# A fused attention and mixture-of-experts layer: expert places read beside v, and the last normalisation split anew between VectorE and GpSimd

## The chip, the core and the metric

The kernel runs on one core of a Trainium2 chip. The time is the device time of one execution in microseconds (us); the median of several executions is given. The engines are named TensorE (PE in the rows; PEld is its weight load), VectorE (DVE), ScalarE (ACT), GpSimd (POOL) and SyncE (SP, which here only issues copies).

## What is computed

Input x is 8 x 256 x 256 in float32, 2048 tokens of 256 features. With `ln` a normalisation over the last axis:

```
x = x + ln(attention(ln(x)))     # 16 query heads, 4 key/value heads of 128; q and k normalised
                                 # and rotated (rope); causal softmax; output projection
x = x + ln(ffn(ln(x)))
ffn: logits = x @ gate_w.T (8 experts); softmax, top 2, weights scaled to sum 1
     out  = sum over the 2 experts of weight * (silu(x @ w_gate) * (x @ w_up)) @ w_down    (176 wide)
     out += sigmoid(x @ shgate_w) * (silu(x @ shw_gate) * (x @ shw_up)) @ shw_down          (352 wide)
```

## The kernel before

Everything is one program per engine, with its order written out by hand; engines meet only at semaphores (`s_...`), each engine runs its own list strictly in order, and a wait in the list holds everything behind it. The float32 products run as three fp32r products of a high and a low part (`mm3`).

**The woven loop.** `for s in range(WOVEN)` (129 steps) carries the attention. A *unit* u (0 to 63) is one key/value head of one 128-token tile; it takes two steps. `qkv(u, y)` on TensorE writes q and k (y = 0: columns 0 to 511 of `pQ`; y = 1: columns 512 to 767, one more head and v). ScalarE squares them for the norm; VectorE's `rope(u, y)` multiplies them by the tables (L1430, L1435; semaphore `s_t2`) and splits v (L1437, `s_v`); GpSimd's `rope(u)` takes a root (L2006, L2008) and finishes with three 128x640 operations (L2020, L2023, L2030; semaphore `s_rope`). Heads follow some steps behind: `scores`, softmax on VectorE and ScalarE, `probs_T`, `pv`, `out_proj`.

**The router.** Tokens are given places in the experts' lists in three chunks of tiles (0 to 9, 10 to 13, 14 to 15). For chunk 0, inside the loop: VectorE finds the two best experts (`route_...`, s = 108 to 117), `route_count(0)` (s = 118; L1624, L1628) sums them, TensorE's `places(0)` (end of s = 118; L672, L679, ten small products into `pA`) makes running counts, `place_read(0)` (s = 119; L1653) reads them, `place_own(0)` (s = 120; L1659, L1662) and `place_ends(0)` (s = 122; L1667, L1669, L1670) write the slots (`s_slots`). One `pv` waits on `s_placed` because it writes the same PSUM bank `pA`. After its last rope GpSimd scatters rows to memory by these slots (L2113), two indirect copies a tile. Expert weights are loaded by SyncE from the moment that the last rope is done (`s_rope`), and converted by ScalarE's `ew_hi` (L1036).

**The feed-forward part and the last normalisation.** From 553 us on, items q walk through the tiles (`ffn(q)` on each engine): 39 routed tiles, then the last five shared ones. Under and behind these comes the end: eight pairs p of tiles, one each q (`PAIR`). For a pair: the two routed rows are added (`last_ysum` on GpSimd, L2147, for p < 5), the shared result is added (`last_sum`, L1731, VectorE; for p = 5 to 7 TensorE makes both sums in PSUM: `pair_results`, `pair_shared`, L755 to L760), `last_stats` (L1740, with L1536 in `norm_aggr`) gives mean and variance, `last_root` on GpSimd gives the scale `lr2` and the offset `nb2` in four operations (L2083, L2085, L2087, L2091), ScalarE's `last_apply` (L1136, semaphore `s_fapp`) applies them, `last_add` on VectorE (L1759) adds the result to x, and SyncE copies the pair out (L449, L452). Pairs 0 and 1, 2 and 3, 4 and 5 share a root, 6 and 7 have their own; pair 7 is scaled and added on VectorE (L1748, L1754) instead.

Names used below: u_lo(m) is L1572, u_act(m) L1568, both VectorE, per shared tile m; out_scale(b) L1491 and out_add(b) L1497; pv_lo L1471, probs_lo L1466; ln2_lo L1550; ew_lo L1510.

## Time and profile before

| what | value |
|---|---|
| median of 3 runs | 680.37 us (679.06 to 681.21) |
| the profiled execution | 683.07 us |
| its span, first to last instruction | 681.0 us |
| mean granted TensorE clock | 0.989 |
| busy: TensorE / VectorE / ScalarE / GpSimd | 631.6 / 567.2 / 564.5 / 552.6 us |

The profile takes one execution; its span leaves out the 2.07 us of start and end. A timeline row is the start of an instruction in us, its duration, engine, line, operation and tiles; where the engine was idle before it, the row ends with that time and with what ended it. Instructions of one engine overlap by some hundredths of a us where they do not depend on each other. A duration is the time from start to completion, waits inside the operation included.

### The profile page before, as it was taken

What the parts mean: (1) busy time and instruction counts of PE and PEld (TensorE: products, weight loads), DVE (VectorE), ACT (ScalarE), POOL (GpSimd) and SP (SyncE); (2) the same over time, 40 slices, a digit from 0 to 9 for tenths busy, and PEclk for the clock granted to TensorE, in tenths of its full rate; (3) what the DMA queues carried; (4) which work ended last, traced back from release to release, by engine and by line L of the source; (5) the groups of instructions that cost most, each with busy time, mean ns of one, the idle gap of its engine ahead of it and who ended that gap; (6) DMA issues with size and microseconds to landing.
All of it is one profiled execution on the core that took longest, in us unless ns stands there. A gap on an engine that the chain in (4) does not pass through costs nothing.

```text
span 681.0 us, 15537 instructions
## 1 busy us (share of the span) xinstructions
PE 631.6 (93%) x4430; PEld 581.0 (85%) x4430; DVE 567.2 (83%) x1925; ACT 564.5 (83%) x2175; POOL 552.6 (81%) x590
## 2 busy tenths in 40 slices
PE   3668999999999999999999999999799999999993
PEld 2557899999999999999999999899688888999981
DVE  6899999998989889888888889999978854555576
ACT  5779999999989999998999999999888535666643
POOL 5799889999999999999999998989866424566654
PEclk9789999999999999999999999999999999999998
DMA  8001113999530000000000000000436124444263
GB/s 336 15 1 33 30 73 118 334 334 276 3 47 1 1 2 2 1 1 2 1 2 1 2 1 2 1 1 25 142 116 203 55 81 116 123 131 119 70 256 124
DMA packets 50978, 54.20 MB, mean 80 GB/s; under 512 B 19824, under 2 KB 42608, under 8 KB 50768
## 3 DMA queue, kind: packets, MB, share of 16 engines
q1 hardware_dynamic: 47488, 43.84, 22.3%
q0 software_dynamic: 3408, 9.38, 3.8%
q8 instruction: 38, 0.62, 0.4%
q14 instruction: 44, 0.36, 0.2%
HBM read 23.76 MB, written 29.51 MB: 78 GB/s over the span
## 4 chain that ended last, share of the span: by engine, by line
POOL 52%; PE 25%; ACT 10%; DVE 6%; issue 4%; DMA 1%; another core or an unknown queue 0%; ACTq 0%; SPq 0%; DVEq 0%; POOLq 0%
POOL ropes L2030 11%; POOL ropes L2020 11%; POOL ropes L2023 9%; POOL rs L2008 9%; PE pQ L459 2%; PE pQ L461 2%; PE pQ L460 2%; POOL hrow L2044 2%; ACT ropes L980 2%; ACT P L995 2%; POOL osb L2051 2%; PE pO L459 2%; POOL rs L2006 2%; POOL lr L2008 1%; PE pO L460 1%
## 5 line engine op out<-in xcount | busy, mean ns | idle before, releaser
L459 PE MATMUL pQ<-W 128*128 128x512 f32 (+2 forms) x334 | 119.3, 357 | 9.6 <-DVE W L1389 5.2
L995 ACT ACTIVATE P<-P,nmx 128x128 f32<-128x128 f32 (+1 forms) x256 | 119.9, 500 | 0.0
L460 PE MATMUL pQ<-W 128*128 128x512 f32 (+2 forms) x334 | 114.4, 342 | 0.0
L461 PE MATMUL pQ<-W 128*128 128x512 f32 (+2 forms) x334 | 113.8, 341 | 0.0
L1003 ACT ACTIVATE P<-P,rinv 128x128 f32<-128x128 f32 (+1 forms) x256 | 107.0, 490 | 1.8 <-DVE rinv L1462 1.6
L2020 POOL TENSOR_TENSOR ropes<-ropes 128x640 f32<-128x640 f32 x63 | 99.2, 1575 | 6.7 <-DVE ropes L1435 6.7
L2030 POOL TENSOR_TENSOR ropes<-ropes 128x640 f32<-128x640 f32 x63 | 100.1, 1589 | 4.9
L980 ACT ACTIVATE ropes<-pQ 128x128 f32<-128x128 f32 x320 | 89.3, 308 | 13.6 <-POOL ropes L2030 7.6
L459 PE MATMUL pO<-W 128*128 128x256 f32 (+1 forms) x323 | 95.1, 295 | 5.4 <-DVE W L1471 3.9
L1466 DVE TENSOR_TENSOR W<-pP,W 128x384 fp32r<-128x384 f32 x128 | 70.2, 548 | 27.6 <-ACT W L1008 27.3
L460 PE MATMUL pO<-W 128*128 128x256 f32 (+1 forms) x323 | 91.5, 283 | 0.0
L461 PE MATMUL pO<-W 128*128 128x256 f32 (+1 forms) x323 | 91.2, 282 | 0.0
L2023 POOL TENSOR_TENSOR ropes<-ropes,rs 128x640 f32<-128x640 f32 x63 | 81.1, 1288 | 4.9
L2008 POOL TENSOR_TENSOR rs<-rs,half 128x5 f32<-128x5 f32 x64 | 77.3, 1207 | 5.3
L459 PEld LDWEIGHTS pQ<-W 128*128 128x128 f32 x334 | 65.3, 195 | 15.9 <-issue 4.5
L980 ACT ACTIVATION_READ_ACCUMULATOR ropes<-pQ 128x1 f32 x320 | 75.2, 241 | 0.0
L459 PEld LDWEIGHTS pO<-W 128*128 128x128 f32 x323 | 61.4, 190 | 12.9 <-DVE W L1471 7.0
L461 PEld LDWEIGHTS pQ<-W 128*128 128x128 f32 x334 | 65.2, 195 | 6.0
L1008 ACT ACTIVATE W<-pP 128x384 fp32r<-128x384 f32 x128 | 67.2, 525 | 2.6 <-PE pP L527 1.4
L460 PEld LDWEIGHTS pQ<-W 128*128 128x128 f32 x334 | 65.7, 197 | 2.9
L2142 POOL DMA_INDIRECT ys<-ropes x39 | 38.8, 995 | 34.1 <-ACT ropes L1131 27.1
L527 PE MATMUL pP<-const,P 128*128 128x128 f32 x384 | 63.2, 274 | 2.0 <-DVE W L1466 1.4
(268 smaller groups left out, 2205.7 us busy)
## 6 DMA issues: line engine op xcount, KB each, us to landing
xs<-stage SPq DMA_DIRECT2D x1, 17550.0 KB, 58.4
stage<-xs SPq DMA_DIRECT2D x39, 130.0 KB
ropes<-in_ew SPq DMA_DIRECT2D x8, 608.0 KB
stage<-in_wqkv SPq DMA_DIRECT2D x3, 768.0 KB, 9.1
stage<-ys SPq DMA_DIRECT2D x4, 512.0 KB, 6.3
ropes<-ys SPq DMA_DIRECT2D x4, 512.0 KB, 7.4
out<-X SPq DMA_DIRECT2D x7, 256.0 KB, 2.0
X<-in_wo SPq DMA_DIRECT2D x1, 1536.0 KB, 13.1
```

Of the source, the lines that this page charges most:

```text
L459: e.matmul(out, lh, rh, start=start, stop=False, skip_group_check=True)
L460: e.matmul(out, lh, rl, start=False, stop=False, skip_group_check=True)
L461: return e.matmul(out, ll, rh, start=False, stop=stop, skip_group_check=True)
L980: a = e.activation(t2[:, z, h * D:h * D + D], pQ[:, h * D:h * D + D], ACT.Square, accum_out=ss[:, z, h:h + 1])
L995: a = e.activation(P[:, z, span(t)], P[:, z, span(t)], ACT.Exp, bias=nmx[:, z, t:t + 1], scale=-1.0, accum_out=sums[:, z, t:t + 1])
L1003: a = e.activation(P[:, z, span(t)], P[:, z, span(t)], ACT.Copy, scale=rinv[:, z, t:t + 1])
L1008: e.activation(PT[:, 0, n % 2, :], pP[:, 0:384], ACT.Copy).then_inc(s_PThi, 1)
L1466: e.tensor_tensor(PT[:, 1, n % 2, :], pP[:, 0:384], f(PT[:, 0, n % 2, :]), ALU.subtract).then_inc(s_PT, 1)
L2008: e.tensor_tensor(dst, dst, half[:, 0:n], ALU.pow).then_inc(s_root, 1)
L2020: e.tensor_tensor(t1[:, z3, :], t1[:, z3, :], t2[:, z, :], ALU.add).then_inc(s_add, 1)
L2023: e.tensor_tensor(v3, v3, rs[:, z, :].unsqueeze(2).to_broadcast([128, 5, D]), ALU.mult).then_inc(s_mul, 1)
L2030: e.tensor_tensor(v3, v3, TB[:, t, :, :], ALU.add).then_inc(s_rope, 1)
```

## The change

Two independent parts.

1. **Chunk 0 of the router.** `places(0)` goes to TensorE's s = 119, ahead of `qkv(59, 1)`, and writes columns 768 to 847 of `pQ` instead of `pA`; the wait of `pv` on `s_placed` goes. `place_read(0)` goes into VectorE's `rope(59, 1)` at s = 120. `route_count(0)`, `place_own(0)` and `place_ends(0)`, seven operations, go out of the loop to behind `soft_rinv(120)`, ahead of `out_scale(6)`.
2. **The last normalisation.** `last_root` on GpSimd keeps the power alone (one operation for four). VectorE makes variance + eps (`last_var`, right behind the statistics) and, later, the offset (`last_nb`, one operation). The additions to x of pairs 1, 3 and 5 go to GpSimd (`last_add` there), those of 0, 2, 4 and 6 stay on VectorE but at other places.

Names:

```
-COUNT_PV = (COUNT0 - 12) // 2
+UPLACE = (COUNT0 + 1) // 2
+POOLADD = (1, 3, 5)
...
-                for (a, b), p in zip(CHUNKS, (pA, pS[1], pS[1]))]
+                for (a, b), p in zip(CHUNKS, (pQ[:, 768:1024], pS[1], pS[1]))]
```

TensorE, in `qkv`, `pv`, `places` (which moves up in the file, unchanged but for this wait) and the loop:

```
+                if u == UPLACE and y == 1:
+                    places(0)
...
-                if 2 * i + 13 == 119:
-                    e.wait_ge(s_placed, 1)
...
-                if c == 0:
-                    e.wait_ge(s_aT, COUNT_PV)
...
-                if s == COUNT0:
-                    places(0)
```

VectorE, in `rope`, in the loop and behind it:

```
+                if u == UPLACE and y == 1:
+                    place_read(0)
...
-                if s == 119:
-                    place_read(0)
...
-                if s == 118:
-                    route_count(0)
-                if s == 120:
-                    place_own(0)
-                if s == 122:
-                    place_ends(0)
...
             soft_rinv(120)
+            route_count(0)
+            place_own(0)
+            place_ends(0)
             out_scale(6)
```

VectorE, the last normalisation (`last_scale` now raises `s_fsum` instead of `s_fapp`, and `last_add_tile` waits for that):

```
+            def last_var(p, n):
+                z = slice(p % 4, p % 4 + n)
+                if p >= 4:
+                    e.wait_ge(s_fapp, p + n - 4)
+                else:
+                    e.wait_ge(s_h2row, NT)
+                e.wait_ge(s_aggr2, NB + p + n)
+                e.tensor_scalar(lr2[:, z, :], mv2[:, z, :, 1], 1.0, EPS, ALU.mult, ALU.add).then_inc(s_var2, 1)
+
+            def last_nb(p, n):
+                z = slice(p % 4, p % 4 + n)
+                e.wait_ge(s_lr2, NB + root_of(p) + 1)
+                e.scalar_tensor_tensor(nb2[:, z, :], mv2[:, z, :, 0], -1.0, lr2[:, z, :], ALU.mult,
+                                       ALU.mult).then_inc(s_nb2, 1)
...
                     if PAIR[q] < PPE:
                         last_sum(PAIR[q])
+                    if PAIR[q] == 4:
+                        last_nb(2, 2)
                     last_stats(PAIR[q])
+                    if PAIR[q] >= 6:
+                        last_var(PAIR[q], 1)
+                    elif PAIR[q] % 2 == 1:
+                        last_var(PAIR[q] - 1, 2)
...
-                p = PAIR.get(q - 2, 0)
-                if 0 < p < 6 and p % 2 == 1:
-                    last_add(p - 1)
-                    last_add(p)
+                p = PAIR.get(q, 0)
+                if p == 2:
+                    last_nb(0, 2)
+                elif p == 3:
+                    last_add(0)
                 elif p == 6:
-                    last_add(p)
+                    last_add(2)
+                    last_nb(4, 2)
                 elif p == 7:
-                    last_scale(p)
+                    last_nb(6, 1)
+                if PAIR.get(q - 1, 0) == 7:
+                    last_add(4)
+                    last_scale(7)
+                    last_add(6)
                     for t in range(2):
-                        last_add_tile(p, t)
+                        last_add_tile(7, t)
```

GpSimd, `last_root` whole as it was (-) and is, and its three additions, each behind the root of the same q:

```
             def last_root(p, n):
-                k = NB + root_of(p)
-                if p >= 4:
-                    e.wait_ge(s_fapp, p + n - 4)
-                else:
-                    e.wait_ge(s_h2row, NT)
                 z = slice(p % 4, p % 4 + n)
-                e.wait_ge(s_aggr2, NB + p + n)
-                e.tensor_scalar(lr2[:, z, :], mv2[:, z, :, 1], 1.0, EPS, ALU.mult, ALU.add).then_inc(s_var2, 1)
-                if p < NPAIR - 1:
-                    e.tensor_scalar(nb2[:, z, :], mv2[:, z, :, 0], -1.0, None, ALU.mult)
-                e.wait_ge(s_var2, k + 1)
+                e.wait_ge(s_var2, NB + root_of(p) + 1)
                 e.tensor_tensor(lr2[:, z, :], lr2[:, z, :], half[:, 0:2 * n].rearrange("p (a b) -> p a b", a=n),
                                 ALU.pow).then_inc(s_lr2, 1)
-                if p < NPAIR - 1:
-                    e.wait_ge(s_lr2, k + 1)
-                    e.tensor_tensor(nb2[:, z, :], nb2[:, z, :], lr2[:, z, :], ALU.mult).then_inc(s_nb2, 1)
+
+            def last_add(p):
+                e.wait_ge(s_fapp, p + 1)
+                e.tensor_tensor(X[:, 2 * p:2 * p + 2, :], X[:, 2 * p:2 * p + 2, :], yl[p][:, :, 0:HID],
+                                ALU.add).then_inc(s_ysum, 1)
...
+                if p == 3:
+                    last_add(1)
+                elif p == 6:
+                    last_add(3)
+                elif p == 7:
+                    last_add(5)
```

SyncE copies the pairs out in their order still, waiting for the engine that adds each (`s_ysum` for 1, 3 and 5, `s_fres` for the others).

How the change moves instructions. On VectorE just behind the loop stood, from soft_max(121) through soft_rinv(120) to the rinv of head 121:

```order
L1456 ISA P,nmx<-pS,P 128x128
L1456 ISA nmx 128x1
L1462 RECIPROCAL rinv<-sums 128x2
L1491 TENSOR_SCALAR osb<-osb,mv,lr 128x256 x2
L1471 TENSOR_TENSOR W<-pA,W 128x512
L1497 TENSOR_TENSOR X<-X,osb 128x512
L1462 RECIPROCAL rinv<-sums 128x2
```

and now stands:

```order
L1473 RECIPROCAL rinv<-sums 128x2
L1635 TENSOR_REDUCE stage<-oh 128x8
L1639 CAST csum<-stage 128x8
L1662 TENSOR_TENSOR stage<-stage 128x160
L1665 TENSOR_REDUCE stage<-stage 128x20
L1670 TENSOR_SCALAR stage<-stage 128x10
L1672 COPY stage<-stage 128x10
L1673 CAST slots<-stage 128x2x10
L1502 TENSOR_SCALAR osb<-osb,mv,lr 128x256 x2
L1482 TENSOR_TENSOR W<-pA,W 128x512
L1508 TENSOR_TENSOR X<-X,osb 128x512
```

The seven operations of the router's chunk 0 (count, own place, slots) lie between soft_rinv and out_scale (L1491, now L1502), and pv_lo (L1471, now L1482) comes seven operations later.

On VectorE in the last normalisation, from last_stats of pair 3 to the additions of pairs 2 and 3, stood (L1731 last_sum, L1740 and L1536 last_stats, L1759 last_add):

```order
L1572 TENSOR_TENSOR W<-pP,W 128x384
L1731 TENSOR_TENSOR ropes<-ropes 128x2x256
L1740 BN_STATS st<-ropes 128x6 x2
L1536 BN_AGGR mv<-st 128x2 x2
L1759 TENSOR_TENSOR X<-X,stage 128x512 x2
L1731 TENSOR_TENSOR ropes<-ropes,P 128x2x256
L1740 BN_STATS st<-ropes 128x6 x2
L1536 BN_AGGR mv<-st 128x2 x2
L1740 BN_STATS st<-pS 128x6 x2
L1536 BN_AGGR mv<-st 128x2 x2
L1759 TENSOR_TENSOR X<-X,ropes 128x512 x2
```

Now, from u_lo(15) on (L1754 last_var, L1759 last_nb, L1777 last_add; L1734 last_sum, L1743 and L1547 last_stats):

```order
L1583 TENSOR_TENSOR W<-pP,W 128x384
L1759 SCALAR_TENSOR_TENSOR nb<-mv,lr 128x4
L1734 TENSOR_TENSOR ropes<-ropes 128x2x256
L1743 BN_STATS st<-ropes 128x6 x2
L1547 BN_AGGR mv<-st 128x2 x2
L1754 TENSOR_SCALAR lr<-mv 128x4
L1777 TENSOR_TENSOR X<-X,stage 128x512
L1734 TENSOR_TENSOR ropes<-ropes,P 128x2x256
L1759 SCALAR_TENSOR_TENSOR nb<-mv,lr 128x4
L1743 BN_STATS st<-ropes 128x6 x2
L1547 BN_AGGR mv<-st 128x2 x2
L1743 BN_STATS st<-pS 128x6 x2
```

Pair 1's addition is gone, the variance stands ahead of pair 0's addition, and an offset each stands ahead of last_sum(3) and ahead of last_stats(4). In the same way a last_var stands right behind last_stats(1), ahead of u_lo(14).

On GpSimd behind its last indirect copies stood (L2147 last_ysum, the rest last_root of pairs 0, 2, 4 and 6):

```order
L2147 TENSOR_TENSOR stage<-stage 128x2x256 x2
L2147 TENSOR_TENSOR ropes<-ropes 128x2x256 x3
L2083 TENSOR_SCALAR lr<-mv 128x4
L2085 TENSOR_SCALAR nb<-mv 128x4
L2087 TENSOR_TENSOR lr<-lr,half 128x4
L2091 TENSOR_TENSOR nb<-nb,lr 128x4
L2083 TENSOR_SCALAR lr<-mv 128x4
L2085 TENSOR_SCALAR nb<-mv 128x4
L2087 TENSOR_TENSOR lr<-lr,half 128x4
L2091 TENSOR_TENSOR nb<-nb,lr 128x4
```

and now stands, to the end of the program (L2103 the power, L2108 last_add):

```order
L2165 TENSOR_TENSOR stage<-stage 128x2x256 x2
L2165 TENSOR_TENSOR ropes<-ropes 128x2x256 x3
L2103 TENSOR_TENSOR lr<-lr,half 128x4 x2
L2108 TENSOR_TENSOR X<-X,stage 128x512
L2103 TENSOR_TENSOR lr<-lr,half 128x4
L2103 TENSOR_TENSOR lr<-lr,half 128x2
L2108 TENSOR_TENSOR X<-X,ropes 128x512
L2103 TENSOR_TENSOR lr<-lr,half 128x2
L2108 TENSOR_TENSOR X<-X,ropes 128x512
```

Pair 1's addition follows the second power, pair 3's the power of pair 6, pair 5's the power of pair 7.

## Rows read from the trace of the kernel before

**Rows 1.** Busy us (x instructions) in a stretch: PE, PEld, DVE, ACT, POOL; clock, DMA.

```profile
456.00:470.00 14.00, 14.00 (x105) 13.22 (x105) 12.63 (x49) 13.55 (x60) 12.84 (x12) 1.00 0.09 30
```

**Rows 2.** Timeline of GpSimd, 442 to 484 us: start, duration, instruction, [idle before, its releaser].

```profile
442.76 1.17 POOL L2008 TENSOR_TENSOR rs<-rs,half 128x5 f32<-128x5 f32 x1
443.89 1.56 POOL L2020 TENSOR_TENSOR ropes<-ropes 128x640 f32<-128x640 f32 x1
...
450.50 1.55 POOL L2020 TENSOR_TENSOR ropes<-ropes 128x640 f32<-128x640 f32 x1 [0.65 <-DVE ropes L1435]
...
458.81 1.55 POOL L2020 TENSOR_TENSOR ropes<-ropes 128x640 f32<-128x640 f32 x1 [0.68 <-DVE ropes L1435]
...
472.87 1.56 POOL L2020 TENSOR_TENSOR ropes<-ropes 128x640 f32<-128x640 f32 x1 [0.48 <-DVE ropes L1435]
...
482.95 1.54 POOL L2030 TENSOR_TENSOR ropes<-ropes 128x640 f32<-128x640 f32 x1
```

**Rows 3.** Timeline of VectorE, 657 to 677 us.

```profile
657.48 1.10 DVE L1731 TENSOR_TENSOR stage<-stage,ropes 128x512 f32<-128x512 f32 x1
...
659.40 0.25 DVE L1536 BATCH_NORM_AGGREGATE mv<-st 128x2 f32<-128x6 f32 x2
659.57 0.52 DVE L1572 TENSOR_TENSOR W<-pP,W 128x384 fp32r<-128x384 f32 x1
...
662.41 0.56 DVE L1572 TENSOR_TENSOR W<-pP,W 128x384 fp32r<-128x384 f32 x1 [0.18 <-ACT W L1092]
...
664.56 1.26 DVE L1759 TENSOR_TENSOR X<-X,stage 128x512 f32<-128x512 f32 x2
665.73 0.68 DVE L1731 TENSOR_TENSOR ropes<-ropes,P 128x512 f32<-128x512 f32 x1
...
668.39 0.25 DVE L1536 BATCH_NORM_AGGREGATE mv<-st 128x2 f32<-128x6 f32 x2
...
676.21 0.76 DVE L1754 TENSOR_TENSOR X<-X,stage 128x256 f32<-128x256 f32 x2
```

**Rows 4.** Timeline of VectorE, 443 to 460 us: three of the seven moved operations.

```profile
443.97 1.51 DVE L1628 CAST csum<-stage 128x8 fp32r<-128x8 f32 x1
...
451.29 0.95 DVE L1659 TENSOR_TENSOR stage<-stage 128x160 f32<-128x160 f32 x1
...
459.60 0.80 DVE L1667 TENSOR_SCALAR stage<-stage 128x10 f32<-128x10 f32 x1
```

**Rows 5.** Timeline of VectorE at 545 us.

```profile
545.21 0.16 DVE L1667 TENSOR_SCALAR stage<-stage 128x2 f32<-128x2 f32 x1
```

**Rows 6.** Timeline of GpSimd, 655 to 668 us.

```profile
655.41 2.62 POOL L2147 TENSOR_TENSOR ropes<-ropes 128x512 f32<-128x512 f32 x2 [0.34 <-DMA ropes<-ys]
659.34 1.28 POOL L2147 TENSOR_TENSOR ropes<-ropes 128x512 f32<-128x512 f32 x1 [1.31 <-DMA ropes<-ys]
...
661.51 1.04 POOL L2087 TENSOR_TENSOR lr<-lr,half 128x4 f32<-128x4 f32 x1
...
665.88 1.42 POOL L2087 TENSOR_TENSOR lr<-lr,half 128x4 f32<-128x4 f32 x1
```

**Rows 7.** Timeline of TensorE at 454 us.

```profile
454.17 0.47 PE L459 MATMUL pA<-W 128*128 128x512 f32 x1 [0.29 <-DVE W L1550]
```

**Rows 8.** Timeline of VectorE, 482 to 485 us: what follows the last soft_rinv.

```profile
482.16 2.49 DVE L1491 TENSOR_SCALAR osb<-osb,mv,lr 128x256 f32<-128x256 f32 x2
484.57 0.68 DVE L1471 TENSOR_TENSOR W<-pA,W 128x512 fp32r<-128x512 f32 x1
```

**Rows 9.** Timeline of ScalarE at 489 us.

```profile
488.80 1.22 ACT L1036 ACTIVATE W<-ropes 128x1216 fp32r<-128x1216 f32 x1 [0.94 <-DMA ropes<-in_ew]
```

**Rows 10.** Timeline of ScalarE at 672 us.

```profile
671.62 1.09 ACT L1136 ACTIVATE ropes<-ropes,nb,lr 128x256 f32<-128x256 f32 x2 [1.93 <-POOL nb L2091]
```

**Rows 11.** Timeline of GpSimd at 528 us.

```profile
528.25 0.91 POOL L2008 TENSOR_TENSOR lr<-lr,half 128x2 f32<-128x2 f32 x1
```

**Rows 12.** Timeline of VectorE at 528 us.

```profile
528.60 1.16 DVE L1510 TENSOR_TENSOR W<-ropes,W 128x960 fp32r<-128x960 f32 x1
```

More of the change, by code:

```diff
@@ L447, in _ @@
             for p in range(NPAIR - 1):
-                e.wait_ge(s_fres, p + 1)
+                if p in POOLADD:
+                    e.wait_ge(s_ysum, PPE + POOLADD.index(p) + 1)
+                else:
+                    e.wait_ge(s_fres, p // 2 + 1)
                 e.dma_start(out_d[:, 2 * p:2 * p + 2, :], X[:, 2 * p:2 * p + 2, :]).then_inc(s_out, 16)
             for m in (NT - 2, NT - 1):
-                e.wait_ge(s_fres, m - NT + NPAIR + 2)
+                e.wait_ge(s_fres, m - NT + 2 + NPAIR - len(POOLADD))
                 e.dma_start(out_d[:, m:m + 1, :], X[:, m:m + 1, :]).then_inc(s_out, 16)
@@ L475, in ln1_T, with places @@
                 p.then_inc(s_ln1T, 1)
+            def places(c):
+                a, b = CHUNKS[c]
+                e.wait_ge(s_oh, c + 1)
+                if c > 0:
+                    e.wait_ge(s_csum, c)
+                if c == 1:
+                    e.wait_ge(s_max, NHEAD)
+                elif c == 2:
+                    e.wait_ge(s_placed, 2)
+                out = pPos[c]
+                p = e.matmul(out, uptri[:, :], oh[:, a:b, :], start=True, stop=False,
+                             skip_group_check=True)
+                if c > 0:
+                    p = e.matmul(out, ones,
+                                 csum[:, c - 1:c, :].to_broadcast([128, b - a, NE]), start=False, stop=False,
+                                 skip_group_check=True)
+                for t in range(b - a - 1):
+                    p = e.matmul(out[:, t + 1:b - a, :], ones,
+                                 oh[:, a + t:a + t + 1, :].to_broadcast([128, b - a - 1 - t, NE]), start=False,
+                                 stop=t == b - a - 2, skip_group_check=True)
+                p.then_inc(s_pos, 1)
             def qkv(u, y):
@@ L658, in u_down @@
                 p.then_inc(s_udown, 1)
-            def places(c):
-                a, b = CHUNKS[c]
-                e.wait_ge(s_oh, c + 1)
-                if c > 0:
-                    e.wait_ge(s_csum, c)
-                if c == 0:
-                    e.wait_ge(s_aT, COUNT_PV)
-                elif c == 1:
-                    e.wait_ge(s_max, NHEAD)
-                else:
-                    e.wait_ge(s_placed, 2)
-                out = pPos[c]
-                p = e.matmul(out, uptri[:, :], oh[:, a:b, :], start=True, stop=False,
-                             skip_group_check=True)
-                if c > 0:
-                    p = e.matmul(out, ones,
-                                 csum[:, c - 1:c, :].to_broadcast([128, b - a, NE]), start=False, stop=False,
-                                 skip_group_check=True)
-                for t in range(b - a - 1):
-                    p = e.matmul(out[:, t + 1:b - a, :], ones,
-                                 oh[:, a + t:a + t + 1, :].to_broadcast([128, b - a - 1 - t, NE]), start=False,
-                                 stop=t == b - a - 2, skip_group_check=True)
-                p.then_inc(s_pos, 1)
             def counts():
@@ L1421, in rope_end, with place_read @@
                 e.tensor_tensor(v3, v3, TB[:, u % 2, :, :], ALU.add).then_inc(s_rope, 1)
+            def place_read(c):
+                a, b = CHUNKS[c]
+                e.wait_ge(s_pos, c + 1)
+                if c == LASTC:
+                    e.wait_ge(s_cnt, 1)
+                e.tensor_tensor(place[c], pPos[c], ebase.unsqueeze(1).to_broadcast([128, b - a, NE]),
+                                ALU.add).then_inc(s_placed, 1)
             def rope(u, y):
@@ L1646, in ends @@
                 return rows[:, a:b, col:col + 1].rearrange("p t c -> p (t c)")
-            def place_read(c):
-                a, b = CHUNKS[c]
-                e.wait_ge(s_pos, c + 1)
-                if c == LASTC:
-                    e.wait_ge(s_cnt, 1)
-                e.tensor_tensor(place[c], pPos[c], ebase.unsqueeze(1).to_broadcast([128, b - a, NE]),
-                                ALU.add).then_inc(s_placed, 1)
             def place_own(c):
```

6 lines of the change are left out of this document (3 added, 3 removed).

## The prediction

> **What bounds the kernel.** I read the chain of waits first. It runs through GpSimd's rope operations, the last of which ends at 484.49 us [rows 2], which suggests GpSimd as the bound of the woven loop. The busy time by stretch says otherwise: in the 14 us from 456 to 470, TensorE is busy for all 14.00, ScalarE for 13.55, VectorE for 12.63 and GpSimd for 12.84 [rows 1]. So the loop's pace is TensorE's, and GpSimd waits here and there for a rope that VectorE delivers late: 0.65 us at unit 59, 0.68 at 60 and 0.48 at 62 [rows 2]. At the very end the order turns round: from 657 us on VectorE works almost without a gap until its last root, then root, application and addition follow one another, and the last addition ends at 676.97 [rows 3].
>
> A third thing decides this change: operations of VectorE and GpSimd keep each other out of SBUF. The cast of 8 numbers a row, L1628, took 1.51 us, from 443.97 to 445.48, and GpSimd's L2020 ran from 443.89 to 445.45 [rows 2, 4]. L1659 (two SBUF inputs) took 0.95 and ended behind the L2020 that started at 450.50; L1667 (one input, strided) took 0.80 and ended behind the one that started at 458.81 [rows 2, 4]. The same operation on two numbers took 0.16 where nothing was in its way [rows 5]. last_sum(1) took 1.10, of which the free one has 0.68, next to GpSimd's last_ysum that ended at 658.03: so the way was free at 657.90, 0.13 before that end [rows 3, 6]. I use 0.13 throughout. What reads PSUM or is a statistic isn't held.
>
> **Part 1, in the loop.** The ten small products of places(0) move by less than a step in a list in which TensorE has no gap; their cost stays where it was. VectorE loses seven operations, three of which took 1.51 + 0.95 + 0.80 [rows 4]; the other four are short. But VectorE isn't the bound: the one gap of TensorE that they made is the 0.29 at 454.17, a pv that waited for ln2_lo (L1550), late behind place_own [rows 7]. GpSimd's waits at 59 and 60 shrink, and the time is waited at 62 instead, where VectorE itself waits for ScalarE and TensorE. I take **-0.3**. Bounds: 0, and -1.8, the sum of the three waits.
>
> **Part 1, behind the loop.** The seven operations now stand at 482.16, ahead of out_scale(6), while GpSimd is in its last rope operations. out_scale(6) itself was held there: 2.49 us for two short passes, to 484.65, when GpSimd's last rope had ended at 484.49 [rows 2, 8]. The count and the cast fit ahead of it, as one pass did; the product with two inputs is held to 484.36. After that come it and a reduction (some 0.25 each), three small ones (0.1 from start to start, the 0.16 of [rows 5] with its overlap) and both passes of out_scale instead of one (484.65 - 484.36 = 0.3): 0.8 + 0.3 = 1.1 us, so pv_lo(58) starts at 485.7 and not 484.57. Behind it are out_proj(116), probs_T(119) and ScalarE's probs_hi(119); then ScalarE waits anyway, 0.94 us, for the expert weights, whose load only the last rope releases [rows 9]. That covers most of the 1.1. GpSimd's first scatter waits for the slots, some 0.7 later, and its root for ln2 follows four scatters later. The scatter wait isn't in the trace of before. I take **+0.3** for both; bounds 0 (the load covers all) and +0.9 (the scatters pass it on whole).
>
> **Part 2, the end of the kernel.** Times on the clock of before.
> 1. last_var(0) is issued at 659.69, behind the aggregate that ends at 659.65. GpSimd's last_ysum(4) runs from 659.34 to 660.62 [rows 3, 6]. So it is held to 660.49 and u_lo(14) starts at 660.56, not 659.57: **+0.99**. Bounds 0.1 and 1.0.
> 2. u_lo(15) waits for ScalarE, which waits for TensorE's work on tiles 14 and 15: 662.41 becomes 663.40. last_nb(0) adds 0.15, so all from last_sum(3) on is late by 1.14. ScalarE's first application starts as much later, although the root is done.
> 3. The additions of pairs 0 and 1 started at 664.56 and took 1.26 [rows 3]. With 1.14, the wait for the last aggregate's end and last_var(2), 0.1 each, pair 0's starts at 665.9; pair 1's is gone, so last_sum(4) follows at 666.5 instead of 665.73.
> 4. The power of pair 2 has to wait for the addition, to 666.45, and takes 1.04 [rows 6] (before, it took 1.42 behind last_sum(4) [rows 6]): done at 667.49. last_nb(2) stands in VectorE's list ahead of last_stats(4) and waits for it. GpSimd's next operation is pair 1's addition, which waits for nothing any more and starts before the power has ended, as L2020 at 443.89 started 0.04 before the end of its root, L2008 [rows 2]. It takes what last_ysum takes, 1.28 [rows 6], and holds VectorE's two-input offset until 668.61. last_stats(4) starts at 668.75; before, it could when last_sum(4) was through, at 666.45. So last_stats(5) ends at 670.94 and not 668.64 [rows 3]: **+2.30** in all. Bound below: the offset slips in first, and it is +1.2.
> 5. From there the path is shorter. Before, 2.98 us passed from the end of last_stats(5) (668.64) to ScalarE's next application (671.62) [rows 3, 10]. Now: last_var(4), the power at 671.30 to 672.34, under it last_stats(6), then last_add(2) and last_nb(4), so 673.06, 2.12 after 670.94. **-0.86**.
> 6. The rest: last_var(7) comes at 674.04 into pair 3's addition on GpSimd (673.48 to 674.76), held to 674.63; last_nb(6); the power of pair 7 behind last_add(4), done at 676.1; last_scale(7) to 677.1; last_add(6), 0.2 held by pair 5's addition, to 677.9; the two last additions to about 678.6. Before: 676.97. The part behind ScalarE's application is 0.2 longer than before, since the chain now goes over GpSimd's list. The end of part 2 is thus **+1.65** (2.30 - 0.86 + 0.2).
>
> The last copies out leave closer together than before; I price that at nothing and leave it to the range.
>
> **The sum.** -0.3 + 0.3 + 1.65 = +1.65. Against the profiled execution of 683.07 this is 684.7; it lay 2.7 above the median of 680.37, and the median becomes **682.0**. A measurement of this kernel can tell about 0.3%, 2.04 us, from no change: the limits are 678.3 and 682.4. The forecast is no change that can be told, on the slow side.
>
> L1510, with two SBUF inputs, started at 528.60 inside a power of 528.25 to 529.16 and took 1.16, and the power 0.91 [rows 11, 12]: it wasn't held to the power's end, or 529.03 + 1.1 would stand there. So the sum goes without such waits. The Trainium skill has a rule that speaks against this change (SBUF — State Buffer, "Who interferes with whom"): of a GpSimd instruction and a VectorE one with two SBUF inputs, or in the fast mode of tensor_scalar, copy and cast, the first holds the shared ports for its whole instruction. For the long additions the rows agree; for the power they don't. By the rule the sum would be that of the first rival.
>
> **Rivals.**
> - **Powers hold the ports too (slower).** Against it are [rows 11, 12], one case only, with a power of two numbers; for it, that the longer additions do. Then last_sum(4) is held behind the power of pair 2, and pair 1's addition and last_nb(2) follow 0.5 later; last_nb(4) is held 0.6 behind the power of pair 6, and last_sum(2) 0.1 behind the first: +1.2, in all +2.85, 683.2. It decides once a power holds for over 0.4 us, when the sum passes 2.04.
> - **The small ones slip through.** last_var(0) isn't held (it has four numbers a row, where L1667 had ten), and last_nb(2) gets in ahead of the addition. Then 1.0 and 1.1 go: +1.65 - 2.1 = -0.45, 679.9. For it: one of out_scale's two passes found its way between two of GpSimd's operations [rows 8]. Against: L1667, strided too, was held [rows 4].
> - **GpSimd's rope chain is the bound of the loop after all**, and the three waits (1.8) go whole: 1.5 more gain than taken, 680.5, or 678.4 together with the rival before. For it is the chain of waits; against it that TensorE has no gap [rows 1].
> - **The late slots cost more.** GpSimd's scatters are released one by one by VectorE and ScalarE waits for the root behind them; if what lies behind has no slack, +1.2 comes on top of the 0.3: 683.2.
>
> **How the numbers follow.** The forecast 0.45; powers hold 0.15; small ones slip 0.20; rope chain 0.12; late slots 0.08. Around 682.0, with part 1 from -0.6 to +0.9 against the 0 taken and part 2 from +0.9 to +2.3, a good third of the forecast lies above 682.4 (0.16), and nearly all of the first and last rival (0.20): slower 0.36. Below 678.3 is half of the rope case's better half and little of the slipping one: faster 0.07. Within: 0.57. The range 679.3 to 683.9 holds the slipping case and both slow ones with some room.
>
> **What would show it.** Right: last_var(0) of some 0.9 us at 659.7, ending with last_ysum(4); last_nb(2) of over 1 us, ending 0.1 before pair 1's addition on GpSimd; last_stats(4) over 2 us later against last_stats(0) than before; the time from last_stats(5) to the next application 2.1 instead of 3.0; TensorE's gap before pv at the place of 454.17 gone and GpSimd's wait at unit 62 grown; the product of place_own long. Wrong: if last_var(0) and last_nb(2) take 0.2 each, part 2 has no loss. If GpSimd's last rope ends over 1 us earlier than 484.5, the loop was GpSimd's. If last_sum(4) is over 1 us beside a power, the first rival holds.

## The result, and the profile after

The changed kernel takes 682.33 us (median of 20 runs, 680.41 to 683.91), the kernel before in the same comparison 680.53 us: a ratio of 1.0022, with a 95% interval from 1.0013 to 1.0032, or 1.5 us slower (0.9 to 2.2). The forecast was 682.0 and no change that can be told, on the slow side. The number came out right. One step behind it did not, as the experiments show.

The profiled execution took 681.8 us, with a span of 679.8, which is less than the 681.0 of the one profiled before. So ends of work in the two traces can't be compared by the clock. I compare distances between two places of one trace. Timeline of VectorE in the changed kernel, 655 to 675 us (L1754 last_var, L1759 last_nb, L1777 last_add, L1583 u_lo, L1743 last_stats, L1734 last_sum):

```profile
655.84 1.23 DVE L1754 TENSOR_SCALAR lr<-mv 128x4 f32<-128x4 f32 x1
656.98 0.54 DVE L1583 TENSOR_TENSOR W<-pP,W 128x384 fp32r<-128x384 f32 x1
...
657.88 0.68 DVE L1734 TENSOR_TENSOR ropes<-ropes 128x512 f32<-128x512 f32 x1
...
660.32 0.15 DVE L1759 SCALAR_TENSOR_TENSOR nb<-mv,lr 128x4 f32<-128x4 f32 x1
...
662.33 0.68 DVE L1777 TENSOR_TENSOR X<-X,stage 128x512 f32<-128x512 f32 x1
662.93 0.68 DVE L1734 TENSOR_TENSOR ropes<-ropes,P 128x512 f32<-128x512 f32 x1
663.98 1.15 DVE L1759 SCALAR_TENSOR_TENSOR nb<-mv,lr 128x4 f32<-128x4 f32 x1 [0.37 <-POOL lr L2103]
665.05 0.74 DVE L1743 BATCH_NORM_STATS2 st<-ropes 128x6 f32<-128x256 f32 x2
...
666.18 0.76 DVE L1743 BATCH_NORM_STATS2 st<-pS 128x6 f32<-128x256 f32 x2
...
670.48 0.68 DVE L1754 TENSOR_SCALAR lr<-mv 128x2 f32<-128x2 f32 x1
...
672.42 1.00 DVE L1766 TENSOR_SCALAR stage<-pT,mv,lr 128x256 f32<-128x256 f32 x2 [0.60 <-POOL lr L2103]
673.34 0.83 DVE L1777 TENSOR_TENSOR X<-X,stage 128x512 f32<-128x512 f32 x1
674.10 0.75 DVE L1772 TENSOR_TENSOR X<-X,stage 128x256 f32<-128x256 f32 x2
```

The same stretch on GpSimd (L2165 last_ysum, L2103 the power, L2108 last_add):

```profile
654.42 2.63 POOL L2165 TENSOR_TENSOR ropes<-ropes 128x512 f32<-128x512 f32 x2 [1.15 <-DMA ropes<-ys]
657.15 1.04 POOL L2103 TENSOR_TENSOR lr<-lr,half 128x4 f32<-128x4 f32 x1
662.50 1.38 POOL L2103 TENSOR_TENSOR lr<-lr,half 128x4 f32<-128x4 f32 x1 [4.31 <-DVE lr L1754]
663.85 1.26 POOL L2108 TENSOR_TENSOR X<-X,stage 128x512 f32<-128x512 f32 x1
...
669.87 1.26 POOL L2108 TENSOR_TENSOR X<-X,ropes 128x512 f32<-128x512 f32 x1
671.24 1.15 POOL L2103 TENSOR_TENSOR lr<-lr,half 128x2 f32<-128x2 f32 x1
672.36 1.26 POOL L2108 TENSOR_TENSOR X<-X,ropes 128x512 f32<-128x512 f32 x1
```

- Two small operations take over a microsecond, as forecast. last_var(0) ends at 657.07 with last_ysum (657.05). last_nb(2) ends at 665.13 with GpSimd's addition of pair 1 (665.11), which had started 0.03 before the end of the power (663.88). The free last_nb(0) takes 0.15.
- last_sum(2), with two SBUF inputs, started at 657.88, inside the power of 657.15 to 658.19, and took its free 0.68. last_sum(4) ran from 662.93 to 663.61, wholly inside the power of 662.50 to 663.88, and took 0.68 too. Neither power held VectorE. That second power itself, which began beside last_add(0) (662.33 to 663.01), took 1.38 instead of 1.04.
- Before, the time from last_stats(0) (655.65) to last_stats(5) (667.59) was 11.94 us. Now it is 652.16 to 666.18, or 14.02: +2.08 against the forecast +2.30. From the end of last_stats(5), 667.23, to ScalarE's next application at 669.45 there are 2.22 us instead of the 2.98 of [rows 3, 10].

From last_stats(0) to the end of VectorE's last addition there were 21.32 us ([rows 3]: 676.97) and are 22.69: +1.37. That isn't all. The last GpSimd operation of the kernel before, from its timeline:

```profile
673.85 1.05 POOL L2087 TENSOR_TENSOR lr<-lr,half 128x2 f32<-128x2 f32 x1
```

It ended at 674.90, 6.10 us before the span's end of 681.0. GpSimd's last operation now ends at 673.62, 6.18 before the end of 679.8. VectorE's last addition ended 4.03 us before the end of the span and now ends 4.95 before it. The experiments had to say which of the two counts.

The loop, in busy us by engine for 456 to 470 us (columns as in [rows 1]), then GpSimd's waits at units 59, 60 and 62:

```profile
456.00:470.00 14.00, 14.00 (x107) 13.30 (x106) 11.84 (x46) 13.55 (x58) 13.07 (x11) 1.00 0.09 29
```

```profile
451.30 1.56 POOL L2045 TENSOR_TENSOR ropes<-ropes 128x640 f32<-128x640 f32 x1 [0.39 <-DVE ropes L1446]
...
459.47 1.55 POOL L2045 TENSOR_TENSOR ropes<-ropes 128x640 f32<-128x640 f32 x1 [0.53 <-DVE ropes L1446]
...
473.55 1.56 POOL L2045 TENSOR_TENSOR ropes<-ropes 128x640 f32<-128x640 f32 x1 [0.47 <-DVE ropes L1446]
...
483.67 1.58 POOL L2055 TENSOR_TENSOR ropes<-ropes 128x640 f32<-128x640 f32 x1
485.74 1.24 POOL L2131 DMA_INDIRECT xs<-stage,slots  x1 [0.49 <-DVE slots L1673]
```

VectorE is less busy (11.84 instead of 12.63), TensorE as full as ever, and the waits at units 59 and 60 shrink from 0.65 and 0.68 to 0.39 and 0.53. That at unit 62 stays (0.48, now 0.47). TensorE's gap of [rows 7] is gone. The moved operations behind the loop, on VectorE:

```profile
483.53 0.31 DVE L1662 TENSOR_TENSOR stage<-stage 128x160 f32<-128x160 f32 x1
483.87 0.32 DVE L1665 TENSOR_REDUCE stage<-stage 128x20 f32<-128x160 f32 x1
484.11 1.17 DVE L1670 TENSOR_SCALAR stage<-stage 128x10 f32<-128x10 f32 x1
...
485.99 0.68 DVE L1482 TENSOR_TENSOR W<-pA,W 128x512 fp32r<-128x512 f32 x1
```

The product (L1662) slipped in between two GpSimd operations, and the reduction behind it (L1665) wasn't held either. L1670, a tensor_scalar, ended at 485.28, 0.03 behind the last rope's end at 485.25; with the 0.16 that it takes when free [rows 5], it was held to 485.12. pv_lo(58) starts 0.74 after that end, where it was 0.08 in [rows 2, 8].

### The profile page after: what moved, and what is told of

The parts are those of the page before. It is cut to its first block, busy times and chain, and to the rows that moved or that the text cites. A ratio compares the mean times of both kernels' runs of the same rounds, so it can differ in the third digit from the quotient of the medians.

```text
span 679.8 us, 15535 instructions
## 1 busy us (share of the span) xinstructions
PE 630.5 (93%) x4430; PEld 580.9 (85%) x4430; DVE 566.6 (83%) x1931; ACT 565.2 (83%) x2175; POOL 554.4 (82%) x580
## 4 chain that ended last, share of the span: by engine, by line
POOL 63%; PE 20%; issue 6%; ACT 6%; DVE 3%; DMA 1%; SPq 0%; DVEq 0%; POOLq 0%; ACTq 0%
POOL ropes L2045 14%; POOL ropes L2055 14%; POOL ropes L2048 12%; POOL rs L2033 11%; POOL hrow L2069 3%; POOL osb L2076 2%; POOL rs L2031 2%; PE pQ L464 2%; POOL lr L2033 2%; PE pQ L466 2%; PE pQ L465 2%; ACT ropes L981 2%; PE pO L464 1%; PE pA L735 1%; PE pT L707 1%
## 5 line engine op out<-in xcount | busy, mean ns | idle before, releaser
L532 PE MATMUL pT<-const,ropes 128*128 128x128 f32 x320 | 58.0, 280 | 8.3 <-DVE W L1456 7.6
```

## The experiments

Besides the two kernels themselves there were twelve runs, of ten new kernels and once more of the two, each timed against the kernel before on the same chip. "Tail" below is the time from last_stats(0) to the end of VectorE's last addition. "x to G" runs from the start of the last x_lo (639.06 in the trace of before, 635.37 in that of the changed kernel) to the end of GpSimd's last operation; it contains the whole end of the kernel, waits for the gathered rows included. "G to end" and "V to end" run from GpSimd's and VectorE's last ends to the span's end.

| kernel | ratio to before (95%) | x to G | G to end | V to end |
|---|---|---|---|---|
| before, first profile | | 35.84 | 6.10 | 4.03 |
| changed | 1.0022 (1.0013 to 1.0032) | 38.25 | 6.18 | 4.95 |
| p1: part 1 alone | 1.0006 (0.9994 to 1.0018) | 36.36 | 6.16 | 4.08 |
| p2: part 2 alone | 1.0034 (1.0019 to 1.0050) | 38.46 | 6.16 | 4.94 |
| w1 | 1.0024 (1.0008 to 1.0039) | 37.20 | 6.15 | 4.93 |
| v0 | 1.0021 (1.0009 to 1.0033) | 37.33 | 6.17 | 4.95 |
| a0: before again | 0.9994 (0.9981 to 1.0008) | 35.85 | 6.16 | 4.09 |
| after2: changed again | 1.0025 (1.0012 to 1.0038) | 38.21 | 6.12 | 4.90 |
| both | 1.0005 (0.9991 to 1.0018) | 36.55 | 6.14 | 4.92 |
| best | 1.0002 (0.9990 to 1.0013) | 35.61 | 6.08 | 4.87 |
| nc: two copies left out | 1.0015 (0.9992 to 1.0038) | 38.18 | 6.16 | 4.94 |
| lc: before, copies late | 1.0004 (0.9982 to 1.0026) | 36.39 | 6.12 | 4.05 |
| best2 | 0.9955 (0.9932 to 0.9978) | 34.92 | 6.09 | 3.61 |
| gp: before, two powers more | 1.0038 (1.0019 to 1.0057) | 37.76 | 6.17 | 5.86 |

How far does x to G vary by itself? Where the end is that of the kernel before it was 35.84, 35.85, 36.36 (p1) and 36.39 (lc), and 35.99 in gp without its two additional powers. In p1 last_sum(1) was held beside a last_ysum (1.62 us instead of 0.68), which makes its tail 22.12. So a difference of 0.5 us between two of these distances can be chance; the 2.4 us between the kernel before and the changed one isn't.

**p1 and p2, the parts alone.** Both are the kernel before with some hunks of the diff above; p1, in its core, then p2:

```diff
+                if u == UPLACE and y == 1:
+                    places(0)
...
+            route_count(0)
+            place_own(0)
+            place_ends(0)
             out_scale(6)
```

```diff
+POOLADD = (1, 3, 5)
...
+            def last_var(p, n):
...
+            def last_nb(p, n):
```

> Part 1 alone on the kernel before: places(0) beside v and rope(59), the count, own slot and ends behind the last rope; the end of the kernel as it was. My theory: the gap of TensorE and the late slots cancel, so the time is that of the kernel before within 0.5 us (ratio 1.000), and the whole loss of the change lies in part 2. If the late slots are what costs (rival), this kernel is 1 to 1.8 us slower than the one before. If GpSimd's rope chain was the bound, it is 1.2 to 1.8 us faster. In the trace: GpSimd's waits at units 59 and 60 shorter, the first scatter some 0.3 us further behind the last rope.

> Part 2 alone on the kernel before: GpSimd's last roots as the power alone, the additions of pairs 1, 3 and 5 on GpSimd; the loop as it was. My theory: all of the loss is here, 1.3 to 1.8 us slower than the kernel before (ratio 1.0019 to 1.0026), and the stretch from last_stats(0) to the last addition is 22.6 to 23.0 us where it was 21.3. If the late slots are what costs, this kernel takes the time of the one before.

Part 1 alone can't be told from the kernel before, part 2 alone costs 2.3 us (1.3 to 3.4). The loss is in part 2. Its tail is 22.68 us, as forecast, and yet the 2.3 us lie above the forecast 1.3 to 1.8, though the interval reaches down to them.

**w1, the wait at last_nb(2).**

```diff
                 if p == 3:
+                    e.wait_ge(s_nb2, NB + 2)
                     last_add(1)
```

> The changed kernel with one wait more: GpSimd's last_add(1) waits until last_nb(2) is done, so it can't hold the ports against it. My theory: last_nb(2) takes 0.15 us instead of 1.15, last_stats(4) starts 0.9 us earlier against last_stats(0), and the kernel is 0.7 to 1.0 us faster than the changed one (about 0.9 us above the kernel before). If last_nb(2) is long because it waits for the power and not because of the addition, nothing changes.

VectorE, then GpSimd's addition in w1:

```profile
664.38 0.16 DVE L1759 SCALAR_TENSOR_TENSOR nb<-mv,lr 128x4 f32<-128x4 f32 x1 [0.37 <-POOL lr L2103]
664.46 0.74 DVE L1743 BATCH_NORM_STATS2 st<-ropes 128x6 f32<-128x256 f32 x2
```

```profile
664.62 1.27 POOL L2108 TENSOR_TENSOR X<-X,stage 128x512 f32<-128x512 f32 x1 [0.34 <-DVE nb L1759]
```

The operation that took 1.15 takes 0.16, the same inputs and the same wait for the power ahead of it. Only the addition beside it is gone. The tail is 21.70 instead of 22.69. The ratio, 1.0024, doesn't show the microsecond; its interval of 1 us to either side doesn't exclude it either.

**v0, the wait at last_var(0).**

```diff
-                    elif PAIR[q] % 2 == 1:
+                    elif PAIR[q] % 2 == 1 and PAIR[q] > 1:
                         last_var(PAIR[q] - 1, 2)
...
                 p = PAIR.get(q, 0)
+                if p == 1:
+                    last_var(0, 2)
```

> The changed kernel with last_var(0) issued one step later, behind u_act(15), where GpSimd's last_ysum(4) is through. My theory: last_var(0) takes 0.2 us instead of 1.23, u_lo(14) starts 1.0 us earlier against last_stats(0), and the kernel is 0.7 to 1.1 us faster than the changed one; that also shows in an earlier last_stats(3). If what follows u_lo(14) waits for ScalarE anyway (rival: the 1.0 is hidden), the time stays within 0.3 us of the changed kernel's.

```profile
656.07 0.23 DVE L1754 TENSOR_SCALAR lr<-mv 128x4 f32<-128x4 f32 x1
```

0.23 instead of 1.23, and a tail of 21.68: another 1.0 us, not hidden by ScalarE. Again the ratio is too coarse to show it.

**a0, after2, both, best.** The two kernels once more, beside two that build on w1 and v0. both has the edits of both. best has also the addition of pair 3 on VectorE:

```diff
-POOLADD = (1, 3, 5)
+POOLADD = (1, 5)
...
                 if PAIR.get(q - 1, 0) == 7:
+                    last_add(3)
                     last_add(4)
...
-                elif p == 6:
-                    last_add(3)
```

> The kernel before once more, for a second profile of it and as a measure of what two sets of runs of one kernel differ by. My theory: the 3 us of ScalarE waits put down to another core or an unknown queue, at 506 to 511 us, were a mark of that one profiled execution; from ew_hi(0) to the second slots there are some 25.5 us here instead of 28.6, while the stretch from last_stats(0) to the last addition is again 21.3 (up to 22.1, as in the run with part 1 alone). If those waits belong to the kernel before, 28.6 comes back. The ratio should be 1.000, with 0.001 to either side.

> The changed kernel once more, on the same chip as the two kernels that build on it. My theory: 1.0025 times the kernel before, and from last_stats(0) to the last addition 22.7 us again.

> The changed kernel with both waits taken away: last_var(0) one step later, and GpSimd's last_add(1) behind last_nb(2). My theory: each took 1.0 us off the end of the kernel by itself (22.69 to 21.70 and 21.68 from last_stats(0) to the last addition), and they add: 20.7 us, the time 1.7 to 2.0 us below the changed kernel and at or just below that of the kernel before (ratio 0.999 to 1.001). If one of them only moves a wait to the other's place, 21.7 stays.

> Both waits taken away, and the addition of pair 3 on VectorE, between last_nb(6) and last_add(4), where VectorE waits 0.60 us for the last root anyway. My theory: last_var(7) takes 0.2 us instead of 0.68, the last power isn't queued behind an addition, and from last_stats(0) to the last addition there are 19.9 to 20.1 us: 0.6 to 0.8 less than with both, and 1 us less than the kernel before (ratio 0.998). If VectorE's added 0.68 us isn't hidden by the wait for the root, it is as long as with both.

a0 settles a side question. From ew_hi(0) to the second slots it has 25.31 us, where the first profile of this same program had 28.61, with 3.04 us in its chain put down to "another core or an unknown queue". The changed kernel has 25.45. These waits came with that execution and not with the kernel, which is why its span was the longer one although its median is lower. after2 repeats the changed kernel: 1.0025, tail 22.76. Beside it on the same chip, both is at 1.0005: the two waits together are worth some 1.4 us by the timer and 1.7 us by x to G.

The tail of both is 21.47, and not 20.7: there a last_ysum started late and held last_sum(1) for 1.67 us instead of 0.68, a wait of 1.0 that isn't among the two taken away. best comes out at 20.15 us of tail, just above the forecast 19.9 to 20.1, with these on VectorE:

```profile
668.20 0.17 DVE L1754 TENSOR_SCALAR lr<-mv 128x2 f32<-128x2 f32 x1
668.27 0.15 DVE L1759 SCALAR_TENSOR_TENSOR nb<-mv,lr 128x2 f32<-128x2 f32 x1
668.34 1.28 DVE L1777 TENSOR_TENSOR X<-X,ropes 128x512 f32<-128x512 f32 x2
669.62 0.99 DVE L1766 TENSOR_SCALAR stage<-pT,mv,lr 128x256 f32<-128x256 f32 x2
```

last_var(7) is free, and the wait for the last root has gone whole behind the addition. But with a tail 1.1 us shorter than in a0 (21.23), best is level with the kernel before (1.0002), and not at 0.998. Here the forecasts failed, and the table's last columns say where: in every kernel with part 2 so far the span goes on 4.9 us behind VectorE's last addition, in those without it 4.1.

**nc and lc, are it the copies out?** My first reading of the 0.8 us was that four copies (two of 256 KB, two of 128) now leave together and share the DMA engines. nc is the changed kernel without the copies of pairs 5 and 6, so it leaves those rows of the output unwritten. lc is the kernel before with those two copies held back. nc, then lc:

```diff
-            for p in range(NPAIR - 1):
+            for p in range(NPAIR - 3):
                 if p in POOLADD:
...
-            e.wait_ge(s_out, 16 * (NPAIR + 1))
+            e.wait_ge(s_out, 16 * (NPAIR - 1))
```

```diff
-                e.wait_ge(s_fres, p + 1)
+                e.wait_ge(s_fres, p + 1 if p < 5 else NPAIR)
```

> The changed kernel without the copies out of pairs 5 and 6 (those rows of the output are not written); all else as it is. In all runs with part 2 the span ends 4.9 us behind VectorE's last addition, in those with the end of the kernel before 4.1, and the last copies take 2.1 instead of 1.8 us to land. My theory since those runs: four copies (256, 256, 128, 128 KB) now leave within 1.5 us and share the DMA engines, which move some 387 GB/s without a gap, so the last lands later. Then here the copy of the last tile lands after 1.8 us and the span ends 4.1 us or less behind the last addition, 0.8 us less than the changed kernel in all. If the 0.8 us is something else of part 2 (a rival), 4.9 us stays.

> The kernel before with one thing changed: SP issues the copies out of pairs 5 and 6 only when tile 14's last addition is done, so that they leave together with those of the last two tiles. No engine waits for them. My theory: 768 KB at 387 GB/s are 2.0 us from the first packet on, where the last tile's copy alone was through 1.4 us after its issue; the issues of four copies follow at 0.45 us each. The last copy lands 1.0 to 1.5 us later than before, and the span ends 5.1 to 5.6 us behind the last addition instead of 4.1: 1.0 to 1.5 us slower than the kernel before (ratio 1.0015 to 1.002). If copies close together cost nothing, as the prediction had it, nothing changes.

The reading falls, twice. How long the last tiles' two copies took to land (the line's own view, changed kernel, then nc, then lc):

```profile
DMA to landing us min/median/max: 2.1/2.1/2.2
```

```profile
DMA to landing us min/median/max: 1.7/1.8/1.8
```

```profile
DMA to landing us min/median/max: 2.1/2.2/2.3
```

So copies close together do take 0.3 to 0.4 us longer, as thought. Both expectations reckon with some 387 GB/s without a gap. The packets of the 256 KB copies come near it (2048 bytes in a median of 86 ns on each of 16 DMA engines, 381 GB/s); while the changed kernel's last four copies ran together, from 675.0 to 676.5, it was 358 GB/s. But the span doesn't end with them: nc still has 4.94 us behind VectorE's last addition, and lc, whose last copy is issued at 681.99, 1.04 after VectorE's last end, still has 4.05. What does stay the same in all thirteen profiles so far, that of best2 below included, is the distance from GpSimd's last end to the end of the span, 6.08 to 6.18 us. In the changed kernel GpSimd's last operation isn't the last root any more; it is the addition of pair 5, 1.26 us long, behind it.

**best2.** best, with pairs 1 and 2 added by GpSimd and pairs 4 and 5 by VectorE ahead of the scale. It was made to spread the copies; it also makes the last root GpSimd's last operation again.

```diff
-POOLADD = (1, 5)
+POOLADD = (1, 2)
...
-                    last_add(2)
+                    last_add(3)
                     last_nb(4, 2)
...
-                    last_add(3)
                     last_add(4)
+                    last_add(5)
...
                     last_add(1)
-                elif p == 7:
-                    last_add(5)
+                    last_add(2)
```

> The version with both waits taken away, with GpSimd adding pairs 1 and 2 and VectorE pair 3 in the place of pair 2, and pairs 4 and 5 ahead of last_scale(7), so that the copies out of pairs 3, 4 and 5 leave earlier. My theory: last_var(4) is held 0.3 us by the addition of pair 2, and the addition of pair 5 costs VectorE 0.3 to 0.6 ahead of the scale, so that the stretch from last_stats(0) to the last addition is 20.5 us, 0.4 more than with pair 3 alone on VectorE; but the span ends 4.1 to 4.3 us behind it instead of 4.9. In all 0.3 us below that version and 1 us below the kernel before (ratio 0.9985 to 0.9995). If the copies weren't what cost, it is 0.4 us slower than that version.

```profile
675.97 1.14 POOL L2106 TENSOR_TENSOR lr<-lr,half 128x2 f32<-128x2 f32 x1 [0.83 <-DVE lr L1754]
```

The tail is 20.46 (20.5 was expected), but the span ends 3.61 us behind it and not 4.1 to 4.3: it ends 6.09 behind this power, at 683.2. The ratio is 0.9955 (0.9932 to 0.9978), the only interval here that lies wholly below 1. x to G gives 0.9 us against the first profile, 0.9986, which is just outside that interval; against lc, whose end is that of the kernel before on the same chip (36.39), it gives 1.5 us. On the chip of this comparison the kernel before took 685.8 us and single runs scattered more widely; that best2 is faster than the kernel before is measured; by how much is not settled. The changed kernel itself wasn't timed on that chip; nc, which is nearly the same, was at 1.0015 (0.9992 to 1.0038).

**gp, the test of the new reading.** The kernel before, with two powers on GpSimd behind the last root, whose results nobody reads:

```diff
                 if p < NPAIR - 1:
...
+                else:
+                    for d in range(2):
+                        e.wait_ge(s_lr2, k + 1)
+                        e.wait_ge(s_nb2, k + d)
+                        e.tensor_tensor(nb2[:, z, :], lr2[:, z, :],
+                                        half[:, 0:2].rearrange("p (a b) -> p a b", a=1),
+                                        ALU.pow).then_inc(s_nb2, 1)
```

> The kernel before with two more powers of two numbers a row behind GpSimd's last root; their results are read by nobody, and a power hasn't held VectorE in any run. In all thirteen profiles the span ends 6.08 to 6.18 us behind the end of GpSimd's last operation, while it ends 3.6 to 4.9 us behind VectorE's last addition. My theory: the program's end waits for GpSimd, so the two powers (some 1.1 us each, 2.1 to 2.4 us together) come whole on the span: 6.1 us behind the second of them, some 6.3 us behind VectorE's last addition, and the time is 2.0 to 2.4 us above the kernel before (ratio 1.003). If VectorE's end or the last copies set the span (rival, and what the prediction took), nothing changes: the span ends 4.1 us behind the last addition, and 4 us behind the last power.

GpSimd, VectorE, and the span:

```profile
677.82 1.04 POOL L2087 TENSOR_TENSOR lr<-lr,half 128x2 f32<-128x2 f32 x1
678.94 1.69 POOL L2096 TENSOR_TENSOR nb<-lr,half 128x2 f32<-128x2 f32 x2
```

```profile
680.18 0.76 DVE L1754 TENSOR_TENSOR X<-X,stage 128x256 f32<-128x256 f32 x2
```

```profile
core 0: 686.8 us, clock 0.978
```

The two powers took 1.69 together, and with the 0.08 ahead of them GpSimd ends 1.77 us later. The span ends 6.17 behind them, and 5.86 instead of 4.1 behind VectorE's last addition: +1.77. Nothing that computes the output waits for these powers, VectorE ends before the span's end by more than ever, and the time is 2.6 us longer (1.3 to 3.9). The end of GpSimd's list sets the end of the span.

The trace also shows what lies between. Behind its own list each engine has some instructions that the program gets at its end; they stand under the line that encloses the whole program (`with ExitStack() as ctx:`, L117 of the kernel before and of gp) and aren't counted as busy. From that line's view, kernel before, then gp (an engine's name with a q is its sequencer; nanoseconds, then the start in us):

```profile
L117 POOLq EVENT_SEMAPHORE  x2: 17/17/17, 680.8 to 680.9; - x2
L117 POOLq DRAIN  x1: 6985/6985/6985, 673.8 to 673.8; - x1
L117 DVEq DRAIN  x1: 797/797/797, 676.2 to 676.2; - x1
L117 SPq DRAIN  x1: 7/7/7, 679.1 to 679.1; - x1
L117 DVEq EVENT_SEMAPHORE  x1: 21/21/21, 681.0 to 681.0; - x1
```

```profile
L117 POOLq DRAIN  x1: 6622/6622/6622, 679.9 to 679.9; - x1
L117 SPq DRAIN  x1: 7/7/7, 683.0 to 683.0; - x1
```

GpSimd's DRAIN lasts until 680.8, 5.9 us behind the end of its last power (674.90), and in gp until 686.5, again 5.9 behind (680.63). VectorE's is over at 677.0, and SyncE's at 679.1, just behind the landing of the last copy. The semaphore instructions of all engines come only after GpSimd's. So GpSimd arrives last, and it does in all fourteen profiles: SyncE, which waits for the last copy, is done 1.7 us ahead of it in the kernel before and 0.4 in lc.

## Why the prediction was right, and where it was wrong

**Where the loss is: right.** Part 2 carries it, part 1 is about nothing.

**Part 1 in the loop, -0.3: right.** From the start of unit 46's L2020 (354.53 in the trace of before) to the end of the last rope there are 129.64 to 129.93 us in the nine kernels with part 1 and 129.96 to 130.29 in the five without: means of 129.75 and 130.11, -0.36. The way to it was in part another: I expected GpSimd's wait at unit 62 to grow as those at 59 and 60 shrank, and it stayed. The two shrank by 0.41 us together and TensorE lost its gap of 0.29, and the gain fits either; the runs don't show which of the two engines sets the pace of the loop.

**Part 1 behind the loop, +0.3: right in sum, the terms were too large.** I put pv_lo(58) 1.2 us behind the last rope's end; it came at 0.74, since L1662 slipped in and not it but L1670 was held. The first scatter came 0.49 behind the rope instead of 0.19, +0.3 and not +0.7. From the last rope's end to the last x_lo the two undisturbed kernels without part 1 on the faster chips (a0, p2) have 150.30 and 150.13, the seven with it 150.12 to 150.79, mean 150.37: some +0.15, inside their own scatter.

**Part 2, step 1 (+0.99): right.** last_var(0) took 1.23, and v0 took exactly 1.0 out of the tail.

**Steps 2 to 4 (+2.30 at last_stats(5)): right**, 2.08. w1 shows the cause: the addition and not the power in front of it.

**Step 5 (-0.86): right**, 2.22 us instead of the forecast 2.12, so -0.76.

**Step 6: wrong, and with it what I took for the end.** "The rest: ... the two last additions to about 678.6. Before: 676.97 ... The end of part 2 is thus +1.65." VectorE's end did come as worked out (+1.37). But I had read from the chain of waits that the kernel ends with VectorE's last addition and the copy behind it. The 4 us behind that were never asked about. gp, nc and lc show that GpSimd's last end and 6.1 us fixed set the span's end. Counted from there, part 2 has three terms. The last power ends 20.23 us behind last_stats(0) instead of 19.25 and 19.16: +1.0. The addition of pair 5 is queued behind it: +1.2. And some +0.15 come ahead of last_stats(0). The sum is +2.4 (38.25 against 35.85), where I had +1.65. In my list this addition appeared as "0.2 held by pair 5's addition", a price on VectorE; on its own engine I gave it none.

**The copies out, priced at nothing: right**, though for no reason that I had. They take longer (2.1 instead of 1.8 us to land), but SyncE, which waits for them, is done ahead of GpSimd's DRAIN.

**Why the number was right all the same.** By x to G and the loop the change costs 2.4 - 0.36 + 0.15 = 2.2 us; measured are 1.5 (0.9 to 2.2) and, again, 1.7 (0.8 to 2.6). The forecast 1.65 lies in both intervals, and so, at the edge or inside, does 2.2. Runs of 12 don't part them. That p1 and p2 sum to 2.7 and the change to 1.6 is in the same scatter. The forecast had 0.7 us too little for part 2 (1.65 for 2.4) and was still within 0.2 us of the measured 1.5 and 1.7: as far as this goes, that the number fits is luck.

**The rivals.** Powers hold the ports: fallen, last_sum(2) beside the first power and last_sum(4) inside the second took 0.68 each. Here the trace decides against the rule of the Trainium skill that whichever of GpSimd and VectorE issues first keeps the shared ports for its whole instruction (SBUF — State Buffer, "Who interferes with whom"), as far as powers go. The long additions follow it: w1 and v0 priced each at 1.0. Small ones slip through: fallen for both operations it named, though L1662 did slip in. Rope chain as the bound, with all three waits gained: fallen, p1 isn't 1.2 us faster; but the waits didn't go (1.8 us before, 1.4 now), so this doesn't show that the chain isn't the bound. Late slots: p1's interval alone reaches to 1.2 us slower, where that rival begins; the 0.15 us from the last rope to the last x_lo speak against it.

## What to carry to other kernels

Ask first what ends the span, and look at every engine's last operation and at the DRAIN behind it, not only at the one that writes the output: the chain of waits ended at a VectorE addition here, while work put at the end of GpSimd's list, which nobody waited for, cost its whole length. Of work moved to another engine count its price there as well as what it holds elsewhere, and where a long GpSimd operation can start just ahead of a tiny one on VectorE, order them: a 0.15 us operation that loses by 0.1 us waits for all of it. When the timer can't tell 1 us, as here, distances inside one trace can, and they have to be checked by a kernel that moves only the suspected end.

## What was not expected of the hardware

- The span ends 6.08 to 6.18 us behind GpSimd's last operation in all fourteen profiles, over spans from 676.9 to 686.8 us (the spread of 0.1 comes from the rounding of the span). 5.9 us of it are GpSimd's own DRAIN, which ends 5.90 us behind its last operation in each of them. Why it takes so long the trace doesn't show; VectorE's ends as its last operation does (677.0), SyncE's takes 7 ns. The Trainium skill tells of a barrier at the end that waits until all engines are done (Runtime: NRT & Kernel Launch, "The ~15µs preamble/postamble breakdown"). The trace agrees: the other engines' last semaphore instructions come within 0.1 us behind GpSimd's. SyncE's last copy landed as little as 0.9 us before the end (lc: issued at 681.99, landed some 2.1 later, end 685.0).
- An operation held by GpSimd ends 0.02 to 0.03 us behind the recorded end of the GpSimd operation that holds it (485.28 and 485.25, 657.07 and 657.05, 665.13 and 665.11); with free times of 0.15 to 0.17 it was let go 0.13 to 0.15 before that end. It doesn't matter how small it is: four numbers a row waited as long as ten. And a power that begins beside a VectorE addition is longer itself (1.38 us instead of 1.04).
- The same program gave an execution with 3 us of waits that another one lacked, and on the chips of the last two comparisons the kernel before took 685.8 and 686.5 us where it took 679.8 to 680.5 on the others. In the four profiles from those two chips the stretch from ew_hi(0) to the second slots has 29.2 to 29.4 us, whatever the kernel. A comparison has to run side by side.
